# Layer 3's attention in steps of two heads of a sequence, with VectorE dividing the value sums

## The reference

```python
q, k, v = cproj(Wq), cproj(Wk), cproj(Wv)            # complex, 64 channels per head
qr, kr = q * phase[None], k * phase[None]            # rotation by position
s = jnp.einsum('bihd,bjhd->bhij', qr, jnp.conj(kr)).real
qn = (q.real ** 2 + q.imag ** 2).sum(-1)             # norms; kn the same of k
E = jnp.exp(jnp.clip(-mu[:, None, None] * dt[None], MIN_EXP, 0.0))
maha = jnp.maximum(qn[..., None] + (E * E)[None] * kn[:, :, None, :] - 2.0 * E[None] * s, 0.0) / V[None]
logits = coef * jnp.log1p(maha / nu) - 0.5 * DH_ * jnp.log(V)[None]
A = jax.nn.softmax(jnp.where(causal, logits, -jnp.inf), axis=-1)
out = jnp.einsum('bhij,bjhd->bihd', A, v)            # then y @ Wo
```

## Time and profile before

| | |
|---|---|
| time, median of 3 runs | 3195.63 us (3187.17 to 3196.6) |
| span of the profiled execution, first to last instruction | 3186.6 us |
| its own time beside the span | not recorded apart; the three runs are 0.6 to 10.0 us above this span |
| mean granted TensorE clock | 0.976 of full speed |
| TensorE, VectorE, ScalarE, GpSimd busy | 96%, 75%, 57%, 27% of the span |
| layer 3's attention | from 1614.05 us to the end |
| recurrence of one unit in its steady part | 12.12 us |

### The profile page before, as it was taken

One profiled execution on the slowest core, in us unless ns is written; L12 is line 12 of the kernel. 1 busy time (PEld: TensorE's weight loads), 2 busy tenths in 40 slices (PEclk: granted clock), 3 DMA queues, 4 the chain that ended last, 5 costly groups with the idle time before them and its releaser, 6 DMA issues. The chain is left out here.

```text
span 3186.6 us, 57933 instructions
## 1 busy us (share of the span) xinstructions
PE 3070.1 (96%) x20342; PEld 2412.7 (76%) x20342; DVE 2384.5 (75%) x5016; ACT 1831.2 (57%) x4246; POOL 856.5 (27%) x707
## 2 busy tenths in 40 slices
PE   6999998999999999997899999999999999999998
PEld 5777675666666678785778888888888888888887
DVE  5878776565566555556868888888888888888888
ACT  3455543654655444433756666666666666666666
POOL 2111101100100100002423344443434444343443
PEclk9999998999999999998999999999999999999999
DMA  2000101000000000003001100011100110000100
GB/s 56 2 5 36 45 27 50 1 1 1 1 1 1 1 1 1 1 1 81 1 1 23 23 9 16 21 23 23 23 9 16 21 23 23 10 23 14 23 1 27
DMA packets 43554, 53.08 MB, mean 17 GB/s; under 512 B 8645, under 2 KB 27272, under 8 KB 43272
## 3 DMA queue, kind: packets, MB, share of 16 engines
q1 hardware_dynamic: 39298, 47.02, 5.9%
q10 hardware_dynamic: 3974, 2.37, 0.3%
HBM read 38.63 MB, written 10.75 MB: 15 GB/s over the span
## 5 line engine op out<-in xcount | busy, mean ns | idle before, releaser
L75 PE MATMUL banks<-scratch 128*128 128x128 f32 (+3 forms) x3648 | 715.7, 325 | 11.5 <-ACT scratch L2999 8.9
L75 PEld LDWEIGHTS banks<-scratch 128*128 128x128 f32 x3648 | 482.9, 192 | 77.0 <-issue 60.3
L75 PE MATMUL banks<-lower 128*128 128x128 f32 (+2 forms) x2688 | 506.7, 354 | 1.2 <-DMA lower<-in_L_w2T 0.6
L75 PEld LDWEIGHTS banks<-lower 128*128 128x128 f32 (+1 forms) x2688 | 343.1, 193 | 165.9 <-issue 164.7
L75 PEld LDWEIGHTS banks<-scratch,tb 128*128 128x128 f32 x2560 | 356.6, 191 | 102.1 <-issue 61.7
L75 PE MATMUL banks<-scratch,tb 128*128 128x128 f32 x2560 | 368.5, 275 | 0.0
L3442 POOL TENSOR_TENSOR scratch<-scratch,aT 128x1024 f32<-128x1024 f32 x128 | 358.8, 2803 | 4.5 <-DVE aT L3264 4.5
L83 DVE SCALAR_TENSOR_TENSOR scratch<-scratch,tb 128x512 f32<-128x512 f32 (+3 forms) x512 | 340.1, 706 | 8.4
L3434 POOL TENSOR_TENSOR scratch<-backwards,nn 128x512 f32<-128x512 f32 x128 | 133.3, 1042 | 736.2 <-ACT nn L3354 736.2
L83 DVE SCALAR_TENSOR_TENSOR scratch<-tb,nn,banks 128x512 f32<-128x512 f32 (+3 forms) x512 | 267.8, 544 | 75.8 <-PE banks L75 71.7
L3264 DVE TENSOR_TENSOR aT<-banks,turn 64x1024 f32<-64x1024 f32 x256 | 312.9, 1222 | 5.7
(11 more groups left out here) (422 smaller groups left out, 4957.1 us busy)
## 6 DMA issues: line engine op xcount, KB each, us to landing
tb<-head_rows SPq DMA_DIRECT2D x32, 512.0 KB, 7.0
turn<-head_turns SPq DMA_DIRECT2D x64, 128.0 KB, 2.7
head_turns<-loads SPq DMA_DIRECT2D x16, 256.0 KB, 2.8
head_turns<-rotation SPq DMA_DIRECT2D x16, 256.0 KB, 3.2
xs<-in_x SPq DMA_DIRECT2D x8, 256.0 KB
w<-in_L_Wqk SPq DMA_DIRECT2D x16, 128.0 KB, 2.0
out<-xs SPq DMA_DIRECT2D x8, 256.0 KB, 2.3
lower<-in_L_w3T ACTq DMA_DIRECT2D x1, 1280.0 KB, 9.2
```

Source lines behind the costliest of these rows:

```text
L75: return self.T.matmul(out, lhsT, rhs, start=start, stop=stop, skip_group_check=True)
```

## The change

Units are worked in pairs: a step m is heads 2hp and 2hp + 1 of one sequence (64 steps). The real parts of the two heads fill the 128 partitions of one bank, their imaginary parts the next.

- `project` makes two matmuls for q and two for k, all through banks 2 and 3.
- `products` on VectorE takes both banks at once, over 128 partitions, four times per step; `rotate` on GpSimd is four adds of 512 columns; `square` on ScalarE now reads the rotated values from SBUF, 1024 columns at a time.
- The norms take two stages: `norms` multiplies 32 weight columns (`norm_w`, of which two sum one head's partitions each) with the squares as moving data, into four groups of 32 partitions of bank 2; ScalarE copies them (`lengths`); `sums` then multiplies them with four columns.
- `scores` multiplies each head over its 64 partitions, x = 0 and 1, head 0 into bank 4 and head 1 into bank 5. Pieces are now 3, then 1 and 0, then 2.
- `outputs` moves to VectorE as one product per unit.
- Weights, turns and tables come for two heads at once; the turn tables in memory are stored for two blocks instead of four; some buffers move.

```diff
-            for block, sine in enumerate((s, ns, ns, s)):
+            for block, sine in enumerate((s, ns)):
...
-    PIECES = ((3,), (2,), (1, 0))
+    PIECES = ((3,), (1, 0), (2,))
...
+        def project(m, x):
...
+            if x:
+                k.after(T, k.h_sinq, m + 1)
+            else:
+                k.after(T, k.h_nn, m)
+            for i in range(2):
+                t = k.mm(k.bank(2 + i), hd["w"][:, 2 * x + i, :], k.nT3[:, b, :])
+            t.then_inc(*(k.h_pk if x else k.h_pq).up())
...
-            for i in range(8):
-                x = k.mm(k.bank(7)[:, 384 + i:385 + i], k.squares[:, i * P:(i + 1) * P], k.minus_half[:, 0:1])
+            for i in range(4):
+                t = k.mm(k.bank(2)[32 * i:32 * i + 32, :], k.norm_w[:, :], k.squares[i // 2][:, i % 2, :])
+            t.then_inc(*k.h_nl.up())
+        def sums(m):
...
+            for i in range(TPB):
+                t = k.mm(k.bank(3)[:, 4 * i:4 * i + 4], k.lengths[:, i * P:(i + 1) * P], k.norm_s[:, :])
...
-                k.mm(ps, t["qk"][:, i * P:(i + 1) * P], t["qk"][:, S:S + n], stop=False)
+                for x in range(2):
+                    for e in range(2):
+                        rows = slice(64 * e, 64 * e + 64)
+                        k.mm(k.bank(4 + e)[:, at:at + n], r["qk"][rows, 0, x, i * P:(i + 1) * P],
+                             r["qk"][rows, 1, x, 0:n], start=(x == 0), stop=False)
...
+        def products(m, x, i):
...
+                V.tensor_tensor(k.sines[x], k.bank(2, 2), hd["turn"][:, 1, :].unsqueeze(1).broadcast_to([P, 2, S]),
+                                ALU.mult).then_inc(*(k.h_sink if x else k.h_sinq).up())
...
+                V.tensor_tensor(r["qk"][:, x, :, :], k.bank(2, 2), hd["turn"][:, 0, :].unsqueeze(1).broadcast_to([P, 2, S]),
+                                ALU.mult).then_inc(*(k.h_ck if x else k.h_cq).up())
...
+        def outputs(g):
...
+            V.tensor_tensor(t["o"], k.bank(0).rearrange("p (t c) -> p t c", c=P),
+                            t["rs"][:, :].unsqueeze(2).broadcast_to([P, TPB, P]), ALU.mult).then_inc(*k.h_out.up())
...
+        def square(m, x):
...
+            out = view(k.squares[1][:, 0, S - 1:S], [[S, 2], [-1, S]]) if x else k.squares[0]
+            A.activation(out, r["qk"][:, x, :, :], ACT.Square).then_inc(*(k.h_sk if x else k.h_sq).up())
+        def lengths(m):
...
+            A.activation(k.lengths, k.bank(2), ACT.Identity).then_inc(*k.h_nc.up())
...
+            A, B = r["qk"][:, x, 0, :], r["qk"][:, x, 1, :]
+            G.tensor_tensor(A, A, k.sines[x][:, 1, :], ALU.subtract)
+            G.tensor_tensor(B, B, k.sines[x][:, 0, :], ALU.add).then_inc(*k.h_rot.up())
```

More of the change, by code:

```diff
@@ L3170, in scores @@
+        def scores(m, p):
+            if not 0 <= m < k.PAIRS:
+                return
+            b, hp, r, hd = k.pair(m)
+            k.after(T, k.h_rot, 2 * (m + 1))
+            k.after(T, k.h_dk, 2 * (m + 1))
+            if b == 0:
+                T.wait_ge(k.h_tb[hp % 2].sem, 64 * (hp // 2 + 1))
+            k.after(T, k.h_qn, k.pieces(m, p, 0) - 1)
             at = 0
[L3171 removed]
+            for i in k.PIECES[p]:
                 n = (i + 1) * P
[L3173 to L3178 removed]
@@ new lines, in scores, with flip @@
+                for e in range(2):
+                    dk = k.lanes3[(2 * m + e) % 4]["dk"]
+                    for j in range(i + 1):
+                        t = k.mm(k.bank(4 + e)[:, at + j * P:at + (j + 1) * P],
+                                 hd["tb"][:, e, 3, (i - j) * P:(i - j + 1) * P], dk[:, 3 - j, :], start=False)
+                    if i == k.PIECES[p][-1]:
+                        t.then_inc(*k.h_sc.up())
+                at += n
+        def flip(g, p):
+            if not 0 <= g < k.UNITS:
+                return
+            m, e, t, r, hd = k.unit(g)
+            f = 3 * g + p
+            k.after(T, k.h_exp, k.pieces(m, p, e))
+            k.after(T, k.h_pt, f - 1)
+            at = 0
+            for i in k.PIECES[p]:
+                for j in range(i + 1):
+                    x = k.tr(k.bank(6 + f % 2)[:, at:at + P],
@@ new lines, in logarithm, with exponential @@
+        def logarithm(g, p):
+            if not 0 <= g < k.UNITS:
+                return
+            m, e, t, r, hd = k.unit(g)
+            k.after(A, k.h_y, k.pieces(m, p, e))
+            y = t["y"][:, k.SPAN[p][0]:k.SPAN[p][1]]
+            A.activation(y, y, ACT.Ln, bias=1.0).then_inc(*k.h_ln.up())
+        def exponential(g, p):
+            if not 0 <= g < k.UNITS:
+                return
+            m, e, t, r, hd = k.unit(g)
+            k.after(A, k.h_lg, k.pieces(m, p, e))
+            k.after(A, k.h_rs, g - 3)
+            for i in k.PIECES[p]:
@@ new lines, in heads_act @@
+        for m in range(-4, k.PAIRS + 1):
+            square(m + 2, 0)
+            turned(2 * m, 2)
+            logarithm(2 * m + 3, 0)
+            values(2 * m)
+            square(m + 2, 1)
+            logarithm(2 * m + 2, 1)
+            lengths(m + 2)
+            logarithm(2 * m + 3, 1)
+            exponential(2 * m + 2, 0)
+            norms(m + 2)
+            logarithm(2 * m + 2, 2)
+            values(2 * m + 1)
+            turned(2 * m + 1, 0)
+            exponential(2 * m + 3, 0)
+            logarithm(2 * m + 3, 2)
+            exponential(2 * m + 2, 1)
+            turned(2 * m + 1, 1)
+            exponential(2 * m + 3, 1)
+            turned(2 * m + 1, 2)
+            logarithm(2 * m + 4, 0)
+            exponential(2 * m + 2, 2)
+            turned(2 * m + 2, 0)
+            turned(2 * m + 2, 1)
+            exponential(2 * m + 3, 2)
```

513 lines of the change are left out of this document (240 added, 273 removed).

## The result

| | before | after |
|---|---|---|
| time, median | 3194.81 us (3187.17 to 3196.6) | 3248.8 us (3242.81 to 3250.53) |
| ratio | | 1.0169, 95% interval 1.0148 to 1.0191 |
| span of the profiled execution | 3186.6 us | 3245.9 us |

The account below looks back on a forecast made before the run. TensorE's own passes were taken as the bound, 12.1 us a unit. Steady steps +13, start +12 and end +5 us gave +30 on the median of 3195.63: 3225 us, own range 3205 to 3250 (55%), wider range 3180 to 3290.

Parts of the forecast that it names:

- the hand-over: TensorE's scores of piece 2 wait for VectorE's query norms behind a distance product: 0.10 us per step, bounds 0 and 0.87.
- the start: First waits of TensorE in layer 3's attention: sum 16 us against 3.6 before, so +12 us.
- Work per step: TensorE's work in one two-head step: -3.58 + 0.86 + 0.90 + 1.90 = +0.08 us.
- Column groups side by side: The norms' four column-group matmuls run at once: 0.86 us, bounds 0.86 and 3.44, taken from row groups.
- column rivals: Norms' column groups run one after another (12%): +2.58 us per step, 3390; or two at a time (4%): +0.86, 3280.
- Row halves: 64-row score products of two halves run at once, net 0; rival that they don't (2%): +4.28 us per step, 3499.
- A visit: TensorE going to another array shape and back: 0.39 us for each of four 64-row visits per step, 0.34 for columns.
- The end: VectorE's 11.6 us of closing the sequences begins only after the last values and division: +5 us.
- The other engines: VectorE -1.38 us per step, about 19.5; ScalarE less too; all stay below 24.2 us and are hidden.
- the clash decides: Rival (10%): the distance product beside GpSimd's accumulation costs TensorE the whole 0.87 us each step, +49 us: 3274.
- cheap visits: Rival "Faster" (11%): a shape visit costs 0.10 us in layer 3, the step loses 1.45 us, -93 us: 3132.
- No change: Rival (6%): 0.30 us per shape visit and no stall in the steps: 3195 us.

Follow-up runs that it names:

- squares_early: Kernel after with query norms before the distance product, blocks 1 and 0 multiplied together, norms before block 2's masks, k's squares earlier on ScalarE: 3174.77 us, ratio 0.9938.
- swap_norms: Kernel after with two VectorE items exchanged, the odd head's piece 1 query norms now ahead of its piece 0 distance product: 3216.86 us, ratio 1.0089.
- before_vector_divides: Kernel before with only the division moved: VectorE divides a unit's value sums in one product instead of four ScalarE copies: 3196.13 us, ratio 1.0014.
- three_visits: swap_norms with the 64-row products of blocks 1 and 0 made in a row before both blocks' masks, one shape visit fewer per step: 3194.51 us, ratio 1.0004.
- norms_as_weights: swap_norms with the norms made as before the change, 16 matmuls with squares as weights, no column groups, lengths copy or sums: 3422.8 us, ratio 1.073.
- before_closing_inside: Kernel before with VectorE closing each sequence in the turn behind its last unit instead of all eight at the end: 3198.95 us, ratio 1.0017.

## Why the prediction was right, and by how much it fell short

The direction and the range held, the own range of 3205 to 3250 by 1.2 us only. The sum, 3216.6, was 29 us short of the profiled span: 17 in the steady steps (the hand-over), 7 in the start, 4 that passed before layer 3's attention began, and 2 as the last steps emptied, all rounded. No error made up for another: the two terms that were mis-sized were both too small.

**Work per step**: forecast +0.08 us; the steps without a stall take 24.32 against 24.23, +0.09. Its parts hold as well. Column groups side by side: 0.99 with the entry (forecast 0.86 + about 0.2, less than 1.2 to the next group); the estimate scaled from what the Trainium skill ("TensorE: Matmul & The Clock Gate", section "Measured speedup vs the span model") gives for three groups was 1.08 without the entry, so this trace has more overlap. Both column rivals are out. Row halves: 1.92 us for block 3, just above the forecast 1.7 to 1.9. A visit: 0.39 forecast, 0.40 measured by leaving one out. squares_early shows that the price is one of changing the shape and not of a shape: rows to columns directly saves 23.92 - 23.73 = 0.19 us, half a visit. The Trainium skill, "TensorEngine Tiling (Array Packing)", section "Key Properties", states that a change of tiling mode, not of the tile alone, drains TensorE; this trace agrees in so far as each change has its price.

**The hand-over to the scores of piece 2**: here the step failed, "I take 0.10 per step, bounds 0 and 0.87". The mechanism and the place were right. It is worth 0.47 in 53 steps and 0 in the others: 25 us instead of 6, and swap_norms gave back 26. I had laid durations along the new order and found the wait "about level"; but the partner's start was the thing to place. GpSimd starts its accumulation right behind its rotation, 0.08 us ahead of VectorE's product, so the whole length of one stands ahead of the other. The rival "the clash decides" (the full 0.87) is not reached either, though the product became 1.0 us longer (1.75, where it takes 0.69 undisturbed; the 0.75 of the earlier trace rows that the prediction compared with is a query norms instruction): the first 0.6 us of that fell into VectorE's room. With 25 in place of 6 us the forecast would have been 3244.

**The start**: forecast 12, measured 18.8. The waits are right: 12.3 us more idle time. Left out was that a start full of waits runs partly at the lower clock: that makes up the other 6.5 us, as far as the rows of the start tell.

**The end**: forecast 5, measured 4.8 in the kernel after and 4.5 in before_vector_divides.

**The other engines**: VectorE near 19.5 per step: 19.22 in an early step and 20.83 in a late one, of which 0.68 is the distance product shown above; the rest stays open. Loads showed nothing.

The rival on the other side, cheap visits, fails on three_visits. "No change" fails with it. Of the two ways of being wrong that the prediction named, a column-group time taken from row groups and a visit priced in other surroundings, neither came about.

## What to carry to other kernels

Where TensorE is the bound, count its passes, but price each change of the array's shape (0.2 us, so 0.4 a visit, in float32 here) and then arrange work so that shapes follow each other: with the clash out of TensorE's way (0.8 points), a visit saved (0.85) and two visits joined (0.66), this change went from 1.7% slower to 0.6% faster. Where VectorE has two operands in SBUF, ask what GpSimd starts just ahead of it, and put what TensorE waits for in front of such an instruction. And when an instruction is moved to an earlier place, move what feeds it in the same edit: the one line on ScalarE took the late steps from 24.55 to 23.73 us, and the ratio from 1.0133 to 0.9938.

## What the runs showed of the hardware that I had not expected

- An instruction of VectorE with both operands in SBUF that begins behind one of GpSimd ends 0.53 to 0.55 us after GpSimd's has ended, however long that one is: 1.75 us beside 1.28 of adding, 1.07 beside 0.60 of copying, 2.72 beside 2.77 of rotating, and 0.69 alone. That fits an instruction that stands until the other is through, and not one that runs at a lower pace. The order counts: in the kernel before, GpSimd's adding that began 0.04 us behind VectorE's gate product took 1.75 us instead of 1.28 (at 3177.95). The Trainium skill says so of two SBUF inputs ("SBUF — State Buffer", section "🔬 SBUF: two separate sides": the pair of ports is an exclusive lock held for the whole instruction), and this trace agrees. What I had not expected is that moving 1.35 us of closing into a loop costs 1.46 us a turn through it, in before_closing_inside.
- TensorE's granted clock fell behind 3.5 us of two-column passes in a row, in every step, although the engine had never been idle (norms_as_weights): passes that usually take 1.00, 0.43 and 0.98 us took 1.40, 0.85 and 1.69.
- Four column groups of 32, each with 512 moving float32 columns, are through in 0.99 us with the entry, where one such matmul at full width takes 0.86.
